# W_base split on chip in freed weight slots instead of ahead of time through DRAM, in an adaLN and FFN kernel

## What is computed

```python
q_emb = relu(q @ W3 + b3)                        # 16 x 1024
v_sum = sum(x, axis=tokens)
y     = relu(((n * x + v_sum) * q_emb) @ W2 + b2)
base  = y @ W_base + b_base
h     = [y @ W_router, y @ A_r, y @ A_s]         # 6 + 96 + 16 columns
gates = softmax(h_router); w = its two largest, zero elsewhere
out   = x + base + (h_shared, h_experts * w) @ [B_s, B_r]
```

## Time and profile before

| | |
|---|---|
| median of 3 runs | 1489.84 us (1486.46 to 1490.41) |
| the profiled execution | 1494.6 us, its span 1492.8 us |
| PE | 1441.2 us busy (97%), mean granted clock 0.981 |
| DVE, ACT, POOL | 908.0 (61%), 654.5 (44%), 163.6 us (11%) |
| DMA | 227.78 MB, 153 GB/s over the span |

### The profile page before, as it was taken

The page is one execution under the profiler, slowest core; times in us unless marked ns, Lnnn a source line. Parts: engine busy times, 40 slices in busy tenths (PEclk is TensorE's granted clock), DMA queues, the critical chain, the costliest instruction groups (busy, mean ns, idle before and its releaser), DMA issues.

```text
span 1492.8 us, 18516 instructions
## 1 busy us (share of the span) xinstructions
PE 1441.2 (97%) x6304; PEld 1176.7 (79%) x6304; DVE 908.0 (61%) x1506; ACT 654.5 (44%) x1257; POOL 163.6 (11%) x229
## 2 busy tenths in 40 slices
PE   7779989899999999999999999999999999999999
PEld 3568878788787787887888888888888888888887
DVE  5967657476464664756656756555565665556564
ACT  3465564755747647467443323132232313223230
POOL 2551221221212212121000000000000000000000
PEclk8899999999999999999999999999999999999999
DMA  8143452543625435253683734627163451816342
GB/s 296 57 119 105 146 189 79 164 135 123 187 72 154 154 117 181 76 179 125 261 302 129 229 137 132 209 61 268 64 209 136 133 211 59 268 64 213 133 127 99
DMA packets 132862, 227.78 MB, mean 153 GB/s; under 512 B 15392, under 2 KB 40480, under 8 KB 130976
## 3 DMA queue, kind: packets, MB, share of 16 engines
q1 hardware_dynamic: 132768, 226.60, 45.5%
HBM read 139.51 MB, written 87.03 MB: 152 GB/s over the span
## 4 chain that ended last, share of the span: by engine, by line
PE 68%; DMA 3%; issue 2%; POOL 1%; ACT 1%; DVE 0%; SPq 0%; ACTq 0%; DVEq 0%; POOLq 0%
PE ps L1385 23%; PE ps L1386 23%; PE ps L1387 23%; DMA wb_lo_scratch<-wl 1%; DMA wt<-in_wbase 1%; POOL wl L625 1%; DMA y_scratch<-buf 1%; POOL wh L623 0%; DMA ws<-in_wbase 0%; ACT src L687 0%; PE ps L1493 0%; PE ps L1487 0%; DVE buf_lo L1073 0%; SPq L383 0%; ACT act_hi L721 0%
## 5 line engine op out<-in xcount | busy, mean ns | idle before, releaser
L1385 PE MATMUL ps<-act_hi,w_hi 128*128 128x512 f32 x1792 | 706.9, 394 | 16.7 <-DVE act_lo L989 16.7
L1386 PE MATMUL ps<-act_lo,w_hi 128*128 128x512 f32 x1792 | 702.2, 392 | 0.0
L1387 PE MATMUL ps<-act_hi,w_lo 128*128 128x512 f32 x1792 | 701.9, 392 | 0.0
L1385 PEld LDWEIGHTS ps<-act_hi,w_hi 128*128 128x128 f32 x1792 | 339.9, 190 | 89.2 <-issue 12.2
L1387 PEld LDWEIGHTS ps<-act_hi,w_lo 128*128 128x128 f32 x1792 | 339.4, 189 | 71.8
L1386 PEld LDWEIGHTS ps<-act_lo,w_hi 128*128 128x128 f32 x1792 | 339.7, 190 | 70.0
L721 ACT ACTIVATE act_hi<-src 128x512 fp32r<-128x512 f32 x380 | 233.1, 624 | 262.9 <-PE ps L1387 261.2
L989 DVE TENSOR_TENSOR act_lo<-src,act_hi 128x512 fp32r<-128x512 f32 x320 | 229.7, 724 | 114.1 <-ACT act_hi L721 113.5
L1038 DVE SCALAR_TENSOR_TENSOR buf<-ps,bb_sb,buf 128x512 f32<-128x512 f32 x128 | 96.1, 751 | 171.7 <-PE ps L1387 161.7
L1038 DVE SCALAR_TENSOR_TENSOR buf<-ps,b_sb,buf 128x512 f32<-128x512 f32 x96 | 71.8, 750 | 89.0 <-PE ps L1387 88.5
L740 ACT ACTIVATE yhi<-buf 128x512 fp32r<-128x512 f32 x128 | 80.2, 626 | 78.0 <-PE ps L1387 77.9
(11 more groups left out here) (108 smaller groups left out, 1109.9 us busy)
## 6 DMA issues: line engine op xcount, KB each, us to landing
src<-in_xT SPq DMA_DIRECT2D x224, 256.0 KB, 3.0
y_scratch<-buf SPq DMA_DIRECT2D x128, 256.0 KB, 2.2
src<-y_scratch SPq DMA_DIRECT2D x128, 256.0 KB, 5.0
outT<-buf SPq DMA_DIRECT2D x128, 256.0 KB, 3.7
buf<-in_xT SPq DMA_DIRECT2D x32, 256.0 KB, 4.5
wb_hi_scratch<-wh SPq DMA_DIRECT2D x56, 128.0 KB, 1.9
wb_lo_scratch<-wl SPq DMA_DIRECT2D x56, 128.0 KB, 2.1
w_hi<-wb_hi_scratch SPq DMA_DIRECT2D x7, 1024.0 KB, 5.5
```

The source lines that it names most:

```text
L1385: nc.tensor.matmul(out, wh, a_h, start=start, stop=False, skip_group_check=onto)
L1386: nc.tensor.matmul(out, wh, a_l, start=False, stop=False, skip_group_check=onto)
L1387: return nc.tensor.matmul(out, wl, a_h, start=False, stop=stop, skip_group_check=onto)
```

## The change

W_base is no longer split ahead. The pieces, their buffers and their DRAM copies are gone. In the last pair of stage 1 SP loads raw quadrants, 1 MB each, into weight slots as they become free (`load_quadrant`), also into the high half of a slot where a sum needs two. ACT rounds 128 x 512 tiles into `w_hi` (`wb_high`), DVE subtracts in place into `w_lo` (`wb_low`) and makes the sums (`wb_sum_1` to `wb_sum_4`), all placed by hand between the work of pairs 7 and 8. The low-rank matrix is loaded raw and split likewise. The C12 and C22 stores are issued between the x loads. The projection has a buffer for each half of a pair (`h_sb`), so `copy_h` waits only for the store of its own buffer. SP:

```diff
-        ws = sb("ws", [P, PW], F32, stage1)
-        wt = sb("wt", [P, PW], F32, stage1)
-        wh = sb("wh", [P, PW], F32R, stage1)
-        a_sb = sb("a_sb", [AC, T], F32, stage1)
+        h_sb = [sb("h_b", [AC, T], F32, stage1), sb("h_a", [AC, T], F32, stage1)]
...
+            def store_hw(i, w):
                 sp.wait_ge(hw_ready, gate_no(i, w))
-                sp.dma_start(hw_dram[2 * i + (w == GB)], source[:]).then_inc(hw_stored, 16)
+                sp.dma_start(hw_dram[2 * i + (w == GB)], h_sb[w][:]).then_inc(hw_stored[w], 16)
 
 
             sp.dma_start(cond_sb[:], condT).then_inc(cond_loaded, 16)
...
-                    sp.wait_ge(prep_saved, 32 * len(PIECES))
-                    load_weights(0)
+                    sp.wait_ge(bank_done, group_no(i, 0, H - 1))
+                    load_quadrant(wl_raw[:, 0], Q11, wl_loaded[0])
...
-                if i > 0:
-                    store_hw(i - 1, GB, a_sb)
+                    if j == 1 and i > 0:
+                        store_hw(i - 1, GB)
                 if last:
-                    load_weights(1)
...
                 if last:
-                    load_weights(2)
-                piece_of(0, 3, False)
+                    sp.wait_ge(bank_done, group_no(i, 2, H - 1))
+                    load_quadrant(wl_raw[:, 2], Q21, wl_loaded[2])
+                    load_quadrant(wh_raw[:, 2], Q22, wh_loaded[2])
...
-                for j in range(H):
-                    sp.wait_ge(c12_done, four(i, j))
-                    sp.dma_start(y_dram[2 * i + 1, j], buf1[:, j, :]).then_inc(buf1_stored[j], 16)
-                    if j == 1:
-                        piece_of(2, 0, False)
+                    if k > 0:
+                        sp.wait_ge(c12_done, four(i, k - 1))
+                        sp.dma_start(y_dram[2 * i + 1, k - 1], buf1[:, k - 1, :]).then_inc(buf1_stored[k - 1], 16)
+                sp.wait_ge(c12_done, four(i, H - 1))
+                sp.dma_start(y_dram[2 * i + 1, H - 1], buf1[:, H - 1, :]).then_inc(buf1_stored[H - 1], 16)
                 if last:
-                    load_weights(4)
-                piece_of(2, 1, True)
+                    sp.wait_ge(wb_s1, H)
+                    load_quadrant(wh_raw[:, 2], Q11, wh_loaded[2])
+                    load_quadrant(wl_raw[:, 4], Q12, wl_loaded[4])
...
                 if last:
-                    load_weights(5)
-                piece_of(3, 1, True)
+                    sp.wait_ge(bank_done, group_no(i, 5, H - 1))
+                    load_quadrant(wl_raw[:, 5], Q11, wl_loaded[5])
+                    load_quadrant(wh_raw[:, 5], Q21, wh_loaded[5])
...
-                    load_weights(6)
+                    load_quadrant(wl_raw[:, 6], Q22, wl_loaded[6])
...
-                    sp.dma_start(low_hi[:].bitcast(F32), lowh_dram).then_inc(low_loaded, 16)
-                    sp.dma_start(low_lo[:].bitcast(F32), lowl_dram).then_inc(low_loaded, 16)
+                    sp.dma_start(low_raw[:], bcat).then_inc(low_loaded, 16)
```

POOL, which also loses `piece` and all its calls:

```diff
-            for q, n, raw in ((Q11, 0, r11), (Q12, 1, r12)):
-                for k in range(H):
-                    pool.wait_ge(w2_loaded[H * q + k], 16)
-                    w2_high(n, raw, k)
+            for k in range(H):
+                pool.wait_ge(w2_loaded[H * Q12 + k], 16)
+                w2_high(1, r12, k)
             pool.wait_ge(q_ready, 2)
             shift_of(0, G21)
             for k in range(H):
                 pool.wait_ge(s2_made, k + 1)
                 w2_high(2, s2, k)
+            shift_of(0, G22)
```

ACT; `wb_high(n, j)` is called in pair 7 in the loops of products 3 (n = 0), 4 (1), 6 (3) and of pair 8's product 0 (2), in pair 8 in those of products 2 (4), 5 (5) and 6 (6):

```diff
-                if gate_no(i, w) > 1 and (i, w) != (LAST, GA):
-                    act.wait_ge(hw_stored, 16 * (gate_no(i, w) - 1))
-                out = a_last if (i, w) == (LAST, GA) else a_sb
-                nc.scalar.activation(out[:], ps[0:AC, H_BANK[w], :], ACT.Copy).then_inc(h_copied, 1)
+                if i > 0:
+                    act.wait_ge(hw_stored[w], 16 * i)
+                nc.scalar.activation(h_sb[w][:], ps[0:AC, H_BANK[w], :], ACT.Copy).then_inc(h_copied, 1)
...
+            def first_w2(k):
+                act.wait_ge(w2_loaded[H * Q11 + k], 16)
+                nc.scalar.activation(w_hi[:, 0, k, :], r11[:, k, :], ACT.Copy).then_inc(first_hi_done, 1)
+
+            first_w2(0)
+            first_w2(1)
...
+            for k in range(2, H):
+                first_w2(k)
             for k in range(H):
                 first_hi(k)
+            act.wait_ge(q_sum, 2)
+            nc.scalar.activation(qrow[:, D // 2:D], ps[0:NB, Q_BANK + 1, :], ACT.Copy).then_inc(q_copied, 1)
...
-                x_sum(0, G22, k, late_sum)
+                x_sum(0, G22, k)
+            x_scale(0, G22)
...
+            def wb_high(n, k):
...
+                if n == 3:
+                    act.wait_ge(bank_done, group_no(LAST, 3, H - 1))
+                    act.wait_ge(wb_s1, k + 1)
+                elif n == 2:
+                    act.wait_ge(wb_s2, k + 1)
+                elif n == 4:
+                    act.wait_ge(wb_s4, k + 1)
+                elif n == 5:
+                    act.wait_ge(wb_s3, k + 1)
+                else:
+                    act.wait_ge(wl_loaded[n], 16)
+                nc.scalar.activation(w_hi[:, n, k, :], wl_raw[:, 2 if n == 3 else n, k, :], ACT.Copy
+                                     ).then_inc(wb_hi_done, 1)
```

DVE; `first_w2_low` takes the place of `w2_low(0, r11)`, with k = 2 and 3 between the low parts of product 0, and `condition(1)` comes ahead of `w2_low(1, r12)`:

```diff
-            def late_scale(n, q):
...
-            late_scale(1, G22)
...
+                y_low(0, C11, 0)
+                y_low(0, C11, 1)
                 for k in range(H):
                     nc.vector.tensor_tensor(r21[:, k, :], r11[:, k, :], r21[:, k, :], ALU.subtract).then_inc(s3_made, 1)
-                y_low(0, C11, 0)
-                y_low(0, C11, 1)
...
+            def wb_low(n, k):
+                dve.wait_ge(wb_hi_done, wb_no(n, k))
+                nc.vector.tensor_tensor(w_lo[:, n, k, :], wl_raw[:, 2 if n == 3 else n, k, :],
+                                        w_hi[:, n, k, :].bitcast(F32), ALU.subtract).then_inc(wb_lo_done, 1)
+
+            def wb_sum_1(k):
+                dve.wait_ge(wl_loaded[2], 16)
+                dve.wait_ge(wh_loaded[2], 16)
+                nc.vector.tensor_tensor(wl_raw[:, 2, k, :], wl_raw[:, 2, k, :], wh_raw[:, 2, k, :],
+                                        ALU.add).then_inc(wb_s1, 1)
...
+            def wb_sum_2(k):
+
+                dve.wait_ge(wb_lo_done, wb_no(3, k))
+                dve.wait_ge(wh_loaded[2], 32)
+                nc.vector.tensor_tensor(wl_raw[:, 2, k, :], wl_raw[:, 2, k, :], wh_raw[:, 2, k, :],
+                                        ALU.subtract).then_inc(wb_s2, 1)
...
+            def wb_sum_4(k):
+                dve.wait_ge(wb_s2, k + 1)
+                dve.wait_ge(wl_loaded[4], 16)
+                nc.vector.tensor_tensor(wl_raw[:, 4, k, :], wl_raw[:, 4, k, :], wl_raw[:, 2, k, :],
+                                        ALU.subtract).then_inc(wb_s4, 1)
...
+            def wb_sum_3(k):
+                dve.wait_ge(wl_loaded[5], 16)
+                dve.wait_ge(wh_loaded[5], 16)
+                nc.vector.tensor_tensor(wl_raw[:, 5, k, :], wl_raw[:, 5, k, :], wh_raw[:, 5, k, :],
+                                        ALU.subtract).then_inc(wb_s3, 1)
...
+                    if i == LAST:
+                        for k in range(H):
+                            wb_low(0, k)
...
+                    if i == LAST:
+                        wb_sum_1(j)
+                if i == LAST:
+                    for k in range(H):
+                        wb_low(1, k)
...
+                    if i == LAST:
+                        wb_low(3, j)
                 c22(i, H - 1)
+                if i == LAST:
+                    for k in range(H):
+                        wb_sum_2(k)
                 y_low(i, C22, 0)
...
+                if i == LAST:
+                    for k in range(H):
+                        wb_sum_4(k)
...
+                    if p == 0:
+                        wb_low(2, j)
...
                 c11(g, H - 1)
+                if p == 0:
+                    dve.wait_ge(low_hi_done, 1)
+                    nc.vector.tensor_tensor(low_lo[:], low_raw[:], low_hi[:].bitcast(F32),
+                                            ALU.subtract).then_inc(low_done, 1)
...
+                    if p == 0:
+                        wb_low(4, j)
                 lr_low_b(p)
+                if p == 0:
+                    for k in range(H):
+                        wb_sum_3(k)
...
+                    if p == 0:
+                        wb_low(5, j)
```

PE:

```diff
+            warm(8)
             pe.wait_ge(cond_loaded, 16)
             project(0, range(QK))
+            warm(6)
             pe.wait_ge(const_step, 3)
             turn(0)
+            warm(4)
+            project(1, range(QK))
...
-                        elif g == NP and k == 0:
-                            pe.wait_ge(wb_loaded[n], 32)
+                        elif g == NP:
+                            pe.wait_ge(wb_lo_done, wb_no(n, k))
...
                     elif j == 0:
```

(50 more changed lines are left out.)

229 lines of the change are left out of this document (70 added, 159 removed).

## The result

The kernel after takes 1470.53 us (median of four runs, 1469.64 to 1470.98), the kernel before 1489.34 beside it (1486.46 to 1490.41): a ratio of 0.9876, with a 95% interval of 0.9859 to 0.9893. The profiled execution of after took 1470.98 us, its span 1469.2; before's was 1494.6. The forecast was 1466.1 for the median and 1470.9 for the profiled execution.

What follows compares the result with a forecast made beforehand. TensorE bounds the kernel nearly everywhere; only its gaps and slow-clock stretches can be won back. -19.6 - 8.0 + 2.2 + 1.7 = -23.7 from 1494.6 gives 1470.9 profiled, less 4.8 for the median: 1466.1 us, range 1457 to 1478.

Steps and rivals of the forecast that it cites:

- Pairs 1 to 5: Late y stores go, so these pairs become like pair 6: 95.08 to 91.17 us each, 19.6 us gained (14 to 21.5).
- the gap of 1.7: PE's wait for y_low(C12,1) behind ACT's x_scale of the next G22 and DVE's low(6,1); each pair keeps 1.74 us.
- The opening: Pair 0: casts moved to ACT and project(1) ahead of product 0 start product 2 earlier; 8.0 us gained (3 to 11).
- the second gap: PE's 5.47 us stall in pair 0's C11 projection, behind GpSimd's casts, shift and ACT's scaling; grows to about 6.7.
- the third: PE's 2.24 us gap in pair 0's C12 projection, the ACT chain beside a piece; worth 0.5 less.
- Pairs 7 and 8: Splitting W_base in place costs 2.2 us (0.5 to 8): 0.5 for wb_sum_2, 1.7 for low_lo.
- Clock: One slow stretch behind one of about 8 remaining gaps of 1.7 us, costing 1.7 us.
- rival 1: Slow clock behind each of the 8 kept gaps brings back 12 us: 1478; chance 0.12.
- rivals 2 to 4: GpSimd's opening casts stretch, 1474 (0.12); stores stay late, 1484 (0.07); quadrants land late, 1500 (0.05).
- The sum: Whole kernel: -19.6 - 8.0 + 2.2 + 1.7 = -23.7 from the profiled 1494.6, giving 1470.9.

Runs made afterwards that it cites:

- b_again: The kernel before run again with no edit and a new profile: 1487.14 us, ratio 0.9993; its profiled execution took 1486.53.
- a_pool_shift: After, with GpSimd's small shift for pair 1's G12 placed ahead of the casts for product 5: 1463.64 us, 6.9 under after.
- b_early_stores: Before, with only the C12 and C22 stores issued between the x loads, all pieces kept: 1476.85 us, 11.2 under before (ratio 0.9909).

## Why the prediction was right, and its one wrong step

**Pairs 1 to 5.** Right, against the profile it was worked out from: 91.16 us each where 91.17 was forecast, the gap of 1.7 kept and its chain shown by two edits. What the term didn't say is that 95.08 was not typical of before (93.58 in the second profile).

**The opening.** Forecast 8.0, measured 8.4 in the first profile of after and 10.0 in the second, where product 4 of pair 0 has 1.7 us less of slow clock; the steps ahead of it came out alike in both. Product 1 starts at 30.0 (30), s12 ends at 27.3 (27.6), product 2 starts at 48.05 (48.1), the second gap is 5.96 (6.7; the casts took 6.35 us instead of the 7.37 of the forecast) and the third 1.71 (1.7). Undoing project(1)'s place costs 6.8 us and undoing the four casts 2.1 (0.9 against after's first runs), together about what the opening gave. The second gap's chain, casts, shift and scaling, is shown by moving the shift.

**Pairs 7 and 8.** Gaps of 0.52 and 1.71 where 0.5 and 1.7 were forecast, both at their places. low_lo took 1.22 us; the estimate from rows was 1.2. Pair 7 takes 0.82 us more than in before (89.95 against 89.13) and pair 8 3.54 more, 4.4 together against 2.2 and 1.7 for the clock. No wait of DVE, ACT or PE is ended by a load of W_base: the six into `w_lo`'s slots landed in 6.2 us at the median, the three into `w_hi`'s, which all go out beside another, in 7.7.

**Clock.** One new slow stretch, forecast without a place; it lies behind the gap ahead of product 2 of pair 8. The seven gaps in product 5 of pairs 0 to 6 have none, so rival 1 did not come; rivals 2 to 4 did not either: the casts took 6.35 us and not 15, the stores did not stay late, no quadrant was late.

**The wrong step** is the last: "the median of the runs is 4.8 below it, so 1466.1 us". The sum gave 1470.9 for the profiled execution and 1470.98 was measured, but the median is 1470.5. (The agreement to 0.1 us is in part luck: after's second profiled execution took 1468.86, and the 0.4 us by which the opening gave more than forecast made up for what pairs 7 and 8 cost more.) The 4.8 us were carried over as if they were an offset between a profiled and another execution. The second profile of before shows that such a surplus is made of slow stretches, and to a small part of stalls, of pairs 1 to 5, which the change takes away; without them the runs of after spread over 1.3 us in one set and 3.6 in another, those of before over 8.8. By typical runs of before the pairs were worth some 13 us (the kernel without pieces, by medians; 15.5 by its ratio), not 19.6, and the rest of the sum, -8.0 + 2.2 + 1.7 = -4.1, is what lies between that kernel (1474.98) and after (1470.53): 4.5.

## What to carry over

When the profiled execution is slower than the median, ask whether its surplus is made of what the change removes; if so, don't take it off the sum again, but off the gain. Take a second profile of the baseline before adding up the gains of single edits: a slow stretch that comes and goes is else counted with each of them. What costs in a queue is the place of the one store that someone waits for, not the waiting it does in total. When a step is moved ahead, look at the next one behind the same work, and count with a moved step the group that it now follows.

## What the runs showed of the hardware

**A stall costs more than its gap.** Gaps of 1.73 us cost 2.03 per pair. In after the first matmul behind one and the next two:

```profile
193.97 0.50 PE L1372 MATMUL ps<-yhi,a_hi 128*128 128x512 f32 x1 [1.73 <-DVE buf_lo L1004]
194.30 0.39 PE L1373 MATMUL ps<-buf_lo,a_hi 128*128 128x512 f32 x1
194.53 0.39 PE L1374 MATMUL ps<-yhi,a_lo 128*128 128x512 f32 x1
```

The rows of two matmuls overlap by 0.39 - 0.23 = 0.16 us (their ends are modelled), which a stall takes away before a gap shows: this one starts 2.12 us after the one before, which is 1.89 more than 0.23, for a gap of 1.73. And the first one takes 0.33 to the next instead of 0.23. That is 0.26 of the 0.30.

**The same gap may or may not bring the lower clock.** Behind gaps of 1.70 or 1.71 us ahead of product 2 of pair 8 the clock fell in six of the seven profiles that have it, after's two among them (0.77 over 7.5 us in each), and not in the one with the moved shift, where the window of the same place reads 1.00:

```profile
779.50:787.00 7.50, 5.79 (x29) 4.47 (x28) 6.79 (x14) 1.86 (x4) 0.00 (x0) 1.00 0.21 43
```

Behind the 3.20 us of b_again and the 2.89 of a_pool_shift it stayed at 1.00, behind 2.21 us in pair 6 of b_early_stores it was 0.83 over 10 us and behind 3.77 in the first profile of before 0.66. The gap's length alone doesn't tell. The Trainium skill (TensorE: Matmul & The Clock Gate, Part 1) calls the number of matmuls at the lower level at a kernel's start run-variable. The trace shows the same later in a kernel: with no edit between them, after's two profiles have 0.85 and 0.92 over product 4 of pair 0. Why one place has it nearly always was not found.

**GpSimd shut out by VectorE.** The shift on 4 columns took 0.20 to 0.62 us in after, and 2.82 in a_pool_shift: from 71.96 to 74.78, while DVE ran two y_lows and four sums without a break from 71.03 to 74.71. By the Trainium skill (SBUF — State Buffer, "SBUF: two separate sides") a VectorE instruction with two SBUF inputs holds the shared port pair for its whole length. The trace agrees and shows more: the small instruction did not get in between two of DVE's, each about 0.6 us, but waited for the last of them.
